# Four buffers, paired quotients, a load in quarters and two sets of semaphores in a four-phase kernel on one Trainium2 core

## The reference, cut to what matters

```python
x = x + _layernorm(_L0_attn_ref(_layernorm(x), ...))   # 16 heads of 8, q and k projected to one number per head
x = x + _layernorm(_L0_ffn_ref(_layernorm(x), ...))    # 32 experts, top 4, gated, and a shared expert
x = x + _layernorm(_L1_attn_ref(_layernorm(x), ...))   # rwkv: time mixing, recurrence, channel mixing
x = x + _layernorm(_L1_ffn_ref(_layernorm(x), ...))    # 8 experts, top 2, and a shared expert
```

```python
qc = q_proj - mean(q_proj, axis=1); kc = k_proj - mean(k_proj, axis=1)
std = sqrt(0.5 * (mean(qc ** 2) + mean(kc ** 2)) + 1e-6); q_proj, k_proj = qc / std, kc / std
context = ...       # per query and head: sum over keys of max(q - k, 0) * (v - mean v)
norm = maximum(..., 0.0001)     # 2 * sum over keys of max(q - k, 0) - sum over keys of (q - k)
return 2.0 * context / norm
```

## Time and profile before

| what | value |
|---|---|
| median of 3 runs | 1293.29 us (1292.15 to 1295.11) |
| the profiled execution's own time | 1291.89 us |
| its span, first to last instruction | 1290.1 us |
| mean granted TensorE clock | 0.844 |
| busy: TensorE, its weight loads | 71%, 54% |
| busy: VectorE, ScalarE, POOL | 61%, 49%, 41% |
| attention ends, layer 0 begins | 322.7, 327.5 (4.8 us) |
| layer 0 ends, rwkv begins | 704.8, 709.3 (4.5 us) |
| rwkv ends, layer 1 begins | 953.8, 958.6 (4.8 us) |

### The profile page before, as it was taken

One profiled execution on the slowest core, in us unless ns is written; L12 is line 12 of the kernel. 1 busy time (PEld: TensorE's weight loads), 2 busy tenths in 40 slices (PEclk: granted clock), 3 DMA queues, 4 the chain that ended last, 5 costly groups with the idle time before them and its releaser, 6 DMA issues. The chain is left out here.

```text
span 1290.1 us, 20144 instructions
## 1 busy us (share of the span) xinstructions
PE 914.3 (71%) x5652; PEld 692.4 (54%) x5652; DVE 789.5 (61%) x2400; ACT 630.1 (49%) x1304; POOL 526.9 (41%) x642
## 2 busy tenths in 40 slices
PE   0886666665239988999885546778668999999900
PEld 0642455554228777777674223444447877777700
DVE  4468589998684547334874599998857420018254
ACT  3253677775544223333332656776656545555400
POOL 0001455554126666545770776000004662056074
PEclk9998587777558999999989768888778999999955
DMA  6950000000601125555551211000022132232131
GB/s 173 290 169 1 0 1 0 0 0 1 232 17 46 43 92 151 161 158 153 147 157 57 60 47 41 1 0 1 1 87 83 47 115 79 64 84 75 35 90 47
DMA packets 130723, 96.99 MB, mean 75 GB/s; under 512 B 11600, under 2 KB 121552, under 8 KB 129616
## 3 DMA queue, kind: packets, MB, share of 16 engines
q1 hardware_dynamic: 118352, 70.79, 18.6%
q0 software_dynamic: 12288, 25.19, 6.6%
HBM read 45.61 MB, written 50.33 MB: 74 GB/s over the span
## 5 line engine op out<-in xcount | busy, mean ns | idle before, releaser
L1083 POOL DMA_INDIRECT e_xs<-h_tok,rows_of x128 | 128.7, 1005 | 104.8 <-DVEq L1541 35.4
L1690 DVE COPY e_y_rows<-e_ps_y 128x512 f32<-128x512 f32 x68 | 46.9, 689 | 175.8 <-PE e_ps_y L1280 133.1
L724 ACT ACTIVATE mask<-ps_q,k_neg 128x256 bf16<-128x256 f32 x256 | 100.8, 488 | 33.1 <-PE ps_q L838 33.1
L1096 POOL DMA_INDIRECT e_got<-e_ys,e_rows_of x64 | 65.6, 1025 | 105.8 <-DMA e_ys<-e_y_rows 87.5
L1232 PE MATMUL e_ps_gu<-e_w_all,e_x_turned 128*128 x384 | 96.5, 395 | 2.1 <-ACT e_x_turned L1407 1.7
L1413 ACT ACTIVATE e_silu<-e_ps_gu 128x512 f32<-128x512 f32 x48 | 28.7, 598 | 134.1 <-PE e_ps_gu L1232 134.1
L838 PE MATMUL ps_q<-q_parts,pick 128*128 (+1 forms) x256 | 56.1, 357 | 51.3 <-DVE mask L636 44.6
L1418 ACT ACTIVATE e_hidden<-e_ps_up 128x512 f32<-128x512 f32 x80 | 47.8, 597 | 85.9 <-PE e_ps_up L1262 85.9
L2176 POOL DMA_INDIRECT c_got<-e_ys,rows_of x64 | 71.2, 1113 | 41.1 <-POOLq L118 21.9
L1280 PE MATMUL e_ps_y<-e_w_all,e_h_turned 128*128 x640 | 84.5, 275 | 0.0
L1083 POOL DMA_INDIRECT e_xs<-h_tok,e_rows_of x64 | 64.9, 1015 | 47.7 <-issue 17.1
(11 more groups left out here) (391 smaller groups left out, 2372.5 us busy)
## 6 DMA issues: line engine op xcount, KB each, us to landing
e_x_rows<-e_xs SPq DMA_DIRECT2D x68, 256.0 KB, 3.2
e_ys<-e_y_rows SPq DMA_DIRECT2D x68, 256.0 KB, 2.4
e_xs<-zeros SPq DMA_DIRECT2D x2, 6144.0 KB, 34.2
e_w_all<-in_w SPq DMA_DIRECT2D x4, 1536.0 KB, 12.5
e_xs<-zeros SPq DMA_DIRECT2D x2, 2560.0 KB, 27.3
e_w_all<-in_w SPq DMA_DIRECT2D x4, 1024.0 KB, 9.2
e_xs<-h_tok,rows_of POOLq DMA_INDIRECT x128, 2.3
result<-x_tok SPq DMA_DIRECT2D x8, 256.0 KB
```

Source lines behind the costliest of these rows:

```text
L724: last = nc.scalar.activation(mask[u][QS // 2 + j][keys][:, h * T:(h + 1) * T], psq[1][:, h * T:(h + 1) * T], ACT.Sign, bias=k_neg[u][:, k ...
L1083: nc.gpsimd.indirect_dma_start(out=xs[part], out_offset=bass.IndirectOffsetOnAxis(ap=rows_of[:, t * K + k:t * K + k + 1], axis=0), in_=til ...
L1096: nc.gpsimd.indirect_dma_start(out=got[t % GB][:, k * P:(k + 1) * P], out_offset=None, in_=ys[part], in_offset=bass.IndirectOffsetOnAxis(a ...
```

## The change

- x is loaded by four DMAs, each with a semaphore; SyncE waits for none. VectorE takes statistics per quarter, and norms, products and bias additions (`rows_out`) run by halves: the second half's statistics and roots stand between the first half's additions, and TensorE transposes the second half behind its first eight products.
- q's and k's statistics lie in one tile and are merged in one pass.
- `AHEAD` is 4: four `qn`, `kn`, `hi_r` and PSUM targets, the loop's body is four batches, and POOL clears the unused partitions with 8 memsets in place of 4.
- `results` is called in even steps alone, for two batches at once. `sums`, `num` and `n1` double; its chain has six links (the product is the sixth), then four statistics.
- Semaphores: 116 are made ready once. Between phases `phase_over` only moves lists, with no instruction. In layer 0, ahead of its scatters, and at the end of rwkv, POOL clears each semaphore of the phase before and increments it by one (`renew_semaphores`); the next phase but one uses them. `plain_semaphore`s are no longer cleared.
- In layer 0 `down` and `y_out` run two steps behind `gate_up`; column registers are threefold, `LAG` is 6, the combination starts one step later, and there is one step more.

```diff
+XPARTS = 4
...
-            taken.append(nc.alloc_semaphore(f"{name}_{next(serial)}"))
...
-        def clear_semaphores(n):
-            nc.clear_and_free_semaphores(taken + ready)
+            return nc.alloc_semaphore(f"{name}_{next(serial)}")
+        def phase_over():
+            ready.extend(spent)
+            spent[:] = taken
             taken.clear()
-            ready.clear()
-            nc.all_engine_barrier()
-            ready_semaphores(n)
+        def renew_semaphores(pool):
+            for x in spent:
+                pool.sem_clear(x)
+            for x in spent:
+                pool.sem_inc(x, FROM)
...
-        ready_semaphores(100)
+        ready_semaphores(116)
...
-        def norm_rows(dve, src, dst, done, tiles=TPG):
-            with dve.Fori(0, GROUPS) as g:
-                for t in range(TPG):
-                    last = nc.vector.tensor_scalar(
-                        at(dst, g * GW + t * P), at(src, g * GW + t * P),
-                        at(mean, g * TPG + t, 1), at(rstd, g * TPG + t, 1), ALU.subtract, ALU.mult)
-                last.then_inc(done, 1)
...
-            for g in range(GROUPS):
+        def transposes(pe, src, banks, ready, done, evacuated, which):
+            for g in which:
...
+            x_loaded = [semaphore("x_loaded") for _ in range(XPARTS)]
...
-                    sp.dma_start(x_tok[:, :].rearrange("p (b u c) -> p b u c", u=TPB, c=P),
-                                 a["x"].rearrange("b (u p) c -> p b u c", p=P)).then_inc(loaded, 16)
-                    sp.wait_ge(loaded, FROM + 16)
+                    per = NB // XPARTS
+                    for i in range(XPARTS):
+                        sp.dma_start(x_tok[:, i * per * T:(i + 1) * per * T].rearrange("p (b u c) -> p b u c", u=TPB, c=P),
+                                     a["x"][i * per:(i + 1) * per].rearrange("b (u p) c -> p b u c", p=P)).then_inc(
+                                         x_loaded[i], 16)
...
-        clear_semaphores(100)
+        phase_over()
...
+        pstats = sb("pstats", 2 * NB * 6, rows=PR)
...
+        pmeans, pvars, ptmp = (sb(n, 2 * NB, rows=PR) for n in ("pmeans", "pvars", "ptmp"))
...
+                    env["transposes"](pe, h_tok, ps[6:8], rows_ready, fm_ps, fm_sb, range(GPH))
                     pe.wait_ge(weights, FROM + WLOADS * 16)
-                    pe.wait_ge(fm_sb, FROM + GROUPS)
                     hf = h_fm[:, :].rearrange("p (b t l) -> p l b t", t=HI, l=LO)
                     for half in range(2):
+                        pe.wait_ge(fm_sb, FROM + (half + 1) * GPH)
                         if half:
...
+                        if not half:
+                            env["transposes"](pe, h_tok, ps[6:8], rows_ready, fm_ps, fm_sb, range(GPH, GROUPS))
...
+                    mean, rstd, spread = env["mean"], env["rstd"], env["spread"]
...
+                    def row_stats(i, tiles):
+                        if tiles.start == 0:
+                            dve.wait_ge(env["x_loaded"][i], FROM + 16)
+                        for t in range(i * per + tiles.start, i * per + tiles.stop):
+                            nc.vector.bn_stats(env["stats"][:, t * 6:t * 6 + 6],
+                                               x_tok[:, t * P:(t + 1) * P]).then_inc(stats_done, 1)
+                    def row_roots(half):
+                        cols = slice(half * HT, (half + 1) * HT)
+                        dve.wait_ge(stats_done, FROM + (half + 1) * HT)
+                        yield from env["merge_steps"](c, env["stats"][:, half * HT * 6:(half + 1) * HT * 6],
+                                                      mean[:, cols], rstd[:, cols], spread[:, cols], P // 2)
+                        c.mark(nc.vector.tensor_scalar(spread[:, cols], rstd[:, cols], 1.0 / P, LN_EPS, ALU.mult, ALU.add))
+                        yield
+                        c.wait()
+                        yield from env["inverse_root_steps"](c, rstd[:, cols], spread[:, cols], env["root_tmp"][:, 0:HT])
+                    def normed(g):
+                        for t in range(g * TPG, (g + 1) * TPG):
+                            last = nc.vector.tensor_scalar(h_tok[:, t * P:(t + 1) * P], x_tok[:, t * P:(t + 1) * P],
+                                                           mean[:, t:t + 1], rstd[:, t:t + 1], ALU.subtract, ALU.mult)
+                        last.then_inc(rows_ready, 1)
...
+                    def rows_out(n):
...
+                    for i in range(2):
+                        row_stats(i, range(per))
+                    for _ in row_roots(0):
+                        pass
+                    for g in range(GPH):
+                        normed(g)
+                    row_stats(2, range(per))
+                    dve.wait_ge(weights, FROM + WLOADS * 16)
+                    rows_out(0)
+                    row_stats(3, range(per // 2))
+                    rows_out(1)
+                    row_stats(3, range(per // 2, per))
+                    rows_out(2)
+                    for n, _ in enumerate(row_roots(1)):
+                        if n in (5, 10):
+                            rows_out(3 + n // 10)
+                    for g in range(GPH, GROUPS):
+                        normed(g)
+                        if g < GPH + 3:
+                            rows_out(5 + g - GPH)
+                    for n in range(NQ, 2 * NQ):
+                        rows_out(n)
...
+            AHEAD = 4
+            qn, kn = ([tb(f"{n}{u}", T) for u in range(AHEAD)] for n in ("qn", "kn"))
+            hi_r = [tb(f"hi_r{u}", T, F32R, rows=PR) for u in range(AHEAD)]
...
+            sums = tb("sums", 2 * TPB * HEADS * VC)
+            num = tb("num", 2 * T)
+            n1, half_counts = tb("n1", 2 * TPB * HEADS), tb("half_counts", TILES * HEADS)
...
-                    for x in "qk":
-                        env["merge_stats"](c, pstat[x][:, :], pmean[x][:, :], pvar[x][:, :], ptmp[:, :], T // 2)
+                    env["merge_stats"](c, pstats[:, :], pmeans[:, :], pvars[:, :], ptmp[:, :], T // 2)
...
+                    with dve.Fori(0, NB // AHEAD) as b4_:
+                        for u in range(AHEAD):
+                            b_ = b4_ * AHEAD + u
+                            dve.wait_ge(qk_ps, FROM + b4_ * AHEAD + u + 1)
+                            dve.wait_ge(parted, FROM + b4_ * AHEAD + u + 1)
                             nc.vector.tensor_scalar(qn[u][0:PR, :], at(proj["q"], b_ * T, T), at(pmean["q"], b_, 1),
                                                     at(rs, b_, 1), ALU.subtract, ALU.mult)
                             nc.vector.tensor_scalar(kn[u][0:PR, :], at(proj["k"], b_ * T, T), at(pmean["k"], b_, 1),
...
-                    def sums_in(b_):
...
+                                o = ((parity * TPB + u) * HEADS + half * HALF) * VC
...
-                        c = Chain(dve, batch_self, b_ * steps)
-                        dve.wait_ge(sums_out, FROM + b_ + 1)
+                        c = Chain(dve, batch_self, b_ * (steps // 2))
+                        dve.wait_ge(sums_out, FROM + b_ + 2)
...
+                        both = 2 * TPB * HEADS
                         num3 = num[:, :].rearrange("p (h r) -> p h r", r=HD)
-                        c.link(nc.vector.tensor_tensor(n1[:, :], S[:, :, 2 * HD], q, ALU.mult))
+                        c.link(nc.vector.tensor_tensor(n1[:, :], S[:, :, 2 * HD], at(q_tok, b_ * (TPB * HEADS), both),
+                                                       ALU.mult))
...
-                        c.link(nc.vector.tensor_tensor(n1[:, :], n1[:, :],
-                                                       at(half_counts, b_ * (TPB * HEADS), TPB * HEADS), ALU.subtract))
+                        c.link(nc.vector.tensor_tensor(n1[:, :], n1[:, :], at(half_counts, b_ * (TPB * HEADS), both),
+                                                       ALU.subtract))
                         c.link(nc.vector.tensor_scalar(n1[:, :], n1[:, :], 0.5e-4, None, ALU.max))
                         c.link(nc.vector.reciprocal(n1[:, :], n1[:, :]))
+                        dve.wait_ge(num_out, FROM + b_ + 2)
+                        c.link(nc.vector.tensor_tensor(at(y_tok, b_ * T, 2 * T).rearrange("p (h r) -> p h r", r=HD), num3,
+                                                       n1[:, :].unsqueeze(2).broadcast_to([P, both, HD]), ALU.mult))
                         assert c.n == steps, c.n
-                        dve.wait_ge(num_out, FROM + b_ + 1)
-                        nc.vector.tensor_tensor(at(y_tok, b_ * T, T).rearrange("p (h r) -> p h r", r=HD), num3,
...
-                        for t in range(TPB):
+                        for t in range(2 * TPB):
                             nc.vector.bn_stats(at(stats, b_ * (TPB * 6) + t * 6, 6),
                                                at(y_tok, b_ * T + t * P)).then_inc(stats_done, 1)
@@ -677,31 +705,31 @@
...
+                            sums_in(b_ - 1, 1 - parity)
...
-                        if before:
```

(39 more changed lines are left out.)

98 lines of the change are left out of this document (31 added, 67 removed).

## The result

The changed kernel takes **1260.56 us** (median of 4 runs, 1260.29 to 1263.22) against 1294.2 for the kernel before (4 runs, 1292.15 to 1298.09): a ratio of 0.9741, 95% interval 0.9714 to 0.9768. The forecast was 1269.0 with a range of 1254 to 1280. The profiled execution took 1260.63 us, 31.3 less than the one before, where the sum said 24.3 less.

What follows compares the result with a forecast made beforehand. No engine was full; the prediction read stage by stage which wait ends last. Its terms, -8.9 + 0.5 - 1.2 - 6 + 8.7 - 14.1 - 3.3 = -24.3 us, gave 1269.0 us for the median, range 1254 to 1280.

Steps and rivals of the forecast that it cites:

- Start: Load in four and work in halves start the turning at 42.8 instead of 51.74: -8.9 us; added semaphores +0.5.
- 16 norms at 0.31: At the start, VectorE's 16 norms of a half were costed at 0.31 us each, ending at 21.4.
- Merge: Before q and k are prepared, merging their statistics once drops 7 small instructions of 27: -1.2 us.
- Buffers: Preparing q and k with four buffers takes 20.8 us instead of 27.5; some returns in collisions: -6 us.
- 1.4 us a batch: Preparing q and k: VectorE and POOL take turns, setting this period once four batches of lead are used.
- The rival of the lock: Preparing q and k: VectorE and POOL strictly alternate from the first batch; -3.1 instead of -6, 1272 us; chance 0.20.
- Pairs: Mask loop: paired quotients gain nothing after odd batches and lengthen even ones by 1.1 us: +8.7 us in all.
- the pairs pay: Mask loop rival: full TensorE clock after odd batches makes pairs save 12.3 us instead of costing 8.7; 1248 us; chance 0.12.
- Borders: Between phases, clearing and increments leave every engine's path at three borders; POOL's clears, 0.07 us each, stay hidden: -14.1 us.
- both rivals on dear clears: POOL's clears delay layer 0's scatters: at 0.77 us each 1281 us, chance 0.07; at 1.2 us each 1305, chance 0.02.
- Layer 0: Experts' last products two steps later: 3.75 us a quad, 9 us TensorE gap, only the end gains: -3.3 us.
- rwkv and layer 1: The phases after layer 0: no change forecast, 0 us.

Runs made afterwards that it cites:

- e6: Kernel before the change with the start's 32 statistics and 32 norms written out instead of looped; ratio 0.9953.
- e5: Changed kernel with x loaded by one DMA again, halves kept; 1408.4 us on a chip where the kernel before took 1446 us.
- e2: Changed kernel with AHEAD at 2 instead of 4; 1419.0 us on a chip where the kernel before took 1446 us.
- e8: Changed kernel with each pair's broadcast product and four statistics moved behind the next odd step's first masks; 1257.2 us, ratio 0.9713.
- e11: Changed kernel with only each pair's four statistics moved, behind the next even step's first masks; 1401.9 us where the kernel before took 1446 us.
- e0: Changed kernel itself, run again on a chip where the kernel before took 1291.7 us; 1258.65 us, ratio 0.9732.
- e9: e7 with two one-column memsets added behind each pair's statistics; 1304.6 us, run once, where the kernel before took 1291.7 us.
- e10: Changed kernel with its four statistics per pair over 64 of 128 columns; 1259.0 us, run once, where the kernel before took 1291.7 us.
- e3: Changed kernel with layer 0's last products and copies one step behind gate_up instead of two; 1417.7 us where the kernel before took 1446 us.
- e7: Kernel before the change with the paired quotients and their doubled buffers alone; ratio 1.0033, mask loop 170.78 us.
- e1: Changed kernel with quotients after every batch instead of every second one; ratio 0.9667, mask loop 170.25 us.
- e12: Same kernel as e1, run again; 1400.1 us, ratio 0.9673, mask loop 170.38 us, where the kernel before took 1446 us.

## Why the prediction was right

It was right in direction, range and mechanism of most parts; the sum was 7.0 us short.

- *Start* (-8.9, was -11.6, of it +0.5 for semaphores). The step that failed is the durations. "16 norms at 0.31" took the busy time of one instruction in a loop, for instructions that the change writes out (0.26). Up to the first addition that was made up by luck: VectorE is through with 24 statistics and 16 norms at 21.7 instead of 23.3, but waits 3.89 us for a product that was put at about 2, and the addition is out at 26.2 as forecast. Behind it the statistics, small steps, norms and additions of the second half take 13.3 us instead of 15.5, and the last transposition 0.6 instead of 1.1. That unrolling is part of the change wasn't seen at all, and the -8.9 was put down to the load and the halves; e6 shows unrolling to be the largest part: alone it gives 8.1 us, and the split load 4.0 to 4.5. Their sum is over the 11.6 found: the order in halves by itself costs 0.6 to 1 us (e5 against e6: merge at 109.19 against 108.24, first statistics at 14.94 against 14.61) and pays only by letting the load overlap.
- *Merge* (-1.2, was -0.8). Right in kind: the seven instructions went, and the root behind them took 0.2 us longer (3.07 against 2.83).
- *Buffers* (-6, was -7.5; e2: 7.1). "1.4 us a batch" failed: VectorE and POOL don't take strict turns, and ScalarE's own 1.18 us set the pace, near the lower end that the text gave. The rival of the lock asked for 1.45 a batch and fell. The row at 113.65 shows a collision, 0.91 us instead of 0.40, and four batches still take 4.70 us (113.65 to 118.35), less than POOL's 4 x 0.72 and VectorE's 8 x 0.32 together (5.4). The rule of the Trainium skill (SBUF — State Buffer, "SBUF: two separate sides") agrees with the single row and not with the sum.
- *Pairs* (+8.7, was +6.8). The nearest number with the wrong reason, and so luck. "They grow after even batches, where VectorE sets the pace: 3.6 becomes 4.7" failed twice. The pair's quotients take 4.16 us. The 512 columns didn't add 0.27 to the product: over 256 columns it takes 0.97 us beside POOL's work and 0.42 in the loop's last step, where it is alone, over 512 columns 0.98 beside POOL and 0.68 alone (e8), so its 0.97 was the collision's length and not its width's. And TensorE stands right behind VectorE: e11 shows that its chain needs 10.64 of the 10.76 us. In order, a pair costs 20.59 against 20.44 on average over the same windows before, 0.9 us in six pairs, where 7.7 were forecast for the loop. The rest is 2.9 for the steps out of order, 2.3 at the loop's start (24.9 against 22.7 us from the first mask to the second sums, where the same kernel in e0 takes 23.1), neither of which the forecast or its rivals had, and 0.9 at the end, which was forecast at 1.0. That the pairs pay (1248) fell too.
- *Borders* (-14.1, was -14.0). Right, clears at 0.07 us included, and hidden as forecast; both rivals on dear clears fell.
- *Layer 0* (-3.3, was -6.2). The period of 3.75 us, the gap ahead of part 1 and the gain at the end came as described, though TensorE's gap is 5.67 us and not 9. The end was undersized: "four quads drain in 11 instead of 15" was to give 3.3 and gave 4.3; the remaining 1.9 is within the spread of the scatters.
- *rwkv and layer 1* (0, was +1.9). Their code does the same work. rwkv took 244.0 us before and 245.6 in e9, 245.5 after and 240.9, 245.4 and 242.5 in e0, e8 and e10: spread.

Open: what throws the mask loop out of step. Shown is what the two longest even steps of the disorder are made of, collisions of VectorE's quotients with POOL's work. Not shown is why an even step is granted 0.84 instead of 0.68 ahead of them, nor whether a tenth of a microsecond decides it. Of the kernels with paired quotients, the disorder came in all eight executions (after, e0, e2, e3, e5, e8, e9, e10) in which VectorE reached the sums behind an even batch without a wait and a pair took 20.53 us or more; it did not come in the one where a pair took 20.47 (e7), and it stayed away in the middle of the loop where VectorE had 0.5 us to spare (e1, e11, e12). Each is one profiled execution. Open too is the loop's start, which takes 22.7 to 25.0 us from the first mask to the second sums in these traces, the longer ones with a first step at 0.66 to 0.68.

## What to carry to other kernels

Cost a loop by its period, not by the busy time of its instructions: at 0.25 us an instruction, a pass of four lost 0.3 us to the loop's end; 64 instructions written out took 5.3 us less, and the engine behind them 2.0. Where two engines are within a few tenths of a microsecond of each other in a loop, try half a microsecond of slack for the one that isn't the bound: the three kernels here that had it kept their order. When a step grows with no wait in it, look whether VectorE's operations have come to lie beside POOL's; work moved to another place in the loop helps only if it leaves the stretch between the same two waits. Semaphores can be renewed one by one by an idle engine at 0.07 us each, in place of a clear and a barrier that stop all of them for about 5 us; here that was worth 14.0 us over three borders.

## What had not been expected of the hardware

- The granted clock alternates with the loop, 0.83 in odd steps and 0.68 in even ones, and the loop's period settles at 20.47 to 20.49 us a pair in four different kernels (e1, e7, e11, e12), with VectorE's work in it from 16.7 to 18.6 us a pair. The Trainium skill (TensorE: Matmul & The Clock Gate, "HAM oscillation — how this bites in real kernels") tells of a kernel whose clock falls in every pass of its loop because of a wait in it. The trace agrees that the clock can fall once in every round; TensorE's longest pause is 2.7 us in the steps at 0.83 and 2.9 to 3.1 in those at 0.68, and that a pause is the reason no run here shows.
- The same quotient operation takes 0.26 or 0.70 us, by whether it starts behind or beside a subtraction of POOL's, and two such steps out of sixteen cost 1.4 us of the loop.
- On one chip straight-line code of the routed layers and rwkv ran about 15% slower than on the others while the attention's loops did not: from the end of the mask loop to the end of the kernel e12 needed 1094 us and e0 950. Why isn't shown.
